# A two-layer transformer kernel: a third tile turned by VectorE, Q projected in halves, the ratio and V's copy on ScalarE, V's bias folded into the output's bias

## What is computed

```python
Q = einsum('bse,hec->bhsc', X, Wq) + bq;  K = ... Wk + bk;  V = ... Wv + bv
Q1, Q2 = Q[..., :d], Q[..., d:];  K1, K2 = K[..., :d], K[..., d:]
A1 = Q1 @ K1.T * s;  A2 = Q2 @ K2.T * s                  # each 1024 x 1024
P = softmax(A1) - lam * softmax(A2)
O = P @ V;  Y = concat(O) @ Wo + bo
return layernorm(Y) * gamma + beta, scaled by 0.2
```

## Time and profile before

| | |
|---|---|
| median of three runs | 1576.91 us (1574.72 to 3416.54) |
| the profiled execution | 1573.77 us, span of its instructions 1572.0 us |
| TensorE clock granted, mean | 0.967 |
| busy PE / DVE / ACT / POOL | 1439.6 / 1376.4 / 1198.3 / 1003.8 us |
| share of the span | 92% / 88% / 76% / 64% |
| DMA | 110.80 MB, mean 70 GB/s |

### The profile page before, as it was taken

How to read it: one execution, slowest core, us unless ns; L and a number is a source line. 1 busy time by engine, 2 the same in 40 slices (tenths; PEclk the granted TensorE clock), 3 DMA queues, 4 the chain that set the end, 5 groups by cost and what they waited for, 6 DMA issues and landing times.

```text
span 1572.0 us, 28031 instructions
## 1 busy us (share of the span) xinstructions
PE 1439.6 (92%) x10243; PEld 588.5 (37%) x10243; DVE 1376.4 (88%) x2107; ACT 1198.3 (76%) x1911; POOL 1003.8 (64%) x727
## 2 busy tenths in 40 slices
PE   5899999999999999999999999986685999999985
PEld 1434443344434443344334433434541222222223
DVE  6798998999899989999999989988687999999947
ACT  4787888888888888888888888874342888888882
POOL 2999998898898988989889889880032011111112
PEclk9999999999999999999999999997696999999997
DMA  4243433343244323433343333420000110000001
GB/s 126 76 105 92 106 86 82 102 112 90 78 103 110 96 77 104 109 92 85 91 107 105 83 91 93 114 68 1 1 22 21 31 35 15 16 16 16 16 16 34
DMA packets 154641, 110.80 MB, mean 70 GB/s; under 512 B 31381, under 2 KB 142906, under 8 KB 154506
## 3 DMA queue, kind: packets, MB, share of 16 engines
q1 hardware_dynamic: 154378, 108.99, 26.5%
q0 software_dynamic: 128, 0.03, 0.0%
HBM read 53.82 MB, written 34.87 MB: 56 GB/s over the span
## 4 chain that ended last, share of the span: by engine, by line
PE 53%; ACT 14%; DVE 13%; issue 11%; POOL 7%; DMA 1%; SPq 0%; POOLq 0%; ACTq 0%; DVEq 0%
PE PS L1573 14%; PE PS L1585 10%; PE PS L1599 9%; ACT ering L847 7%; PE PS L1980 4%; POOL ering L656 3%; DVE nmx L1152 2%; PE PS L1942 2%; DVE region L1172 2%; PE PS L1632 2%; PE PS L1964 2%; ACT region L871 2%; DVE mxp L1479 2%; ACT ering L1059 2%; POOL ering L655 2%
## 5 line engine op out<-in xcount | busy, mean ns | idle before, releaser
L1152 DVE TENSOR_REDUCE nmx<-PS 128x1 f32<-128x1024 f32 x512 | 620.1, 1216 | 54.4 <-PE PS L1574 53.5
L847 ACT ACTIVATE ering<-PS,nmx 128x1024 f32<-128x1024 f32 x512 | 570.6, 1116 | 109.6 <-DVE nmx L1152 109.5
L656 POOL TENSOR_TENSOR ering<-ering 128x1024 f32<-128x1024 f32 x256 | 604.2, 2360 | 21.4
L1573 PE MATMUL PS<-region 64*128 64x512 f16 x1536 | 405.1, 381 | 20.4 <-ACT ering L847 14.5
L1574 PE MATMUL PS<-region 64*128 64x512 f16 x1536 | 405.2, 381 | 0.0
L655 POOL TENSOR_SCALAR ering<-ering,rho 128x1024 f32<-128x1024 f32 x256 | 287.3, 1122 | 95.2 <-DVE rho L1161 94.5
L1479 DVE TENSOR_REDUCE mxp<-PS 128x2 f32<-128x1024 f32 x256 | 304.2, 1222 | 34.3 <-PE PS L1964 29.9
L1059 ACT ACTIVATE ering<-PS 128x1024 f32<-128x1024 f32 x256 | 259.6, 1024 | 70.0 <-PE PS L1942 64.1
L1585 PE MATMUL PS<-ident,ering 128*128 128x128 f32 x1536 | 251.5, 286 | 15.6 <-ACT t L858 8.1
L1585 PEld LDWEIGHTS PS<-ident,ering 128*128 128x128 f32 x1536 | 161.6, 141 | 201.7 <-issue 73.8
L1573 PEld LDWEIGHTS PS<-region 64*128 64x128 f16 x1536 | 112.6, 94 | 261.3 <-ACT ering L847 110.2
(11 more groups left out here) (301 smaller groups left out, 1876.2 us busy)
## 6 DMA issues: line engine op xcount, KB each, us to landing
ptd<-t SPq DMA_DIRECT2D x256, 128.0 KB, 2.4
region<-region SPq DMA_DIRECT2D x64, 256.0 KB, 3.5
t<-ptd SPq DMA_DIRECT2D x44, 256.0 KB, 3.5
region<-ptd SPq DMA_DIRECT2D x44, 256.0 KB, 3.5
va<-ptd SPq DMA_DIRECT2D x20, 256.0 KB, 3.4
acc<-ptd SPq DMA_DIRECT2D x20, 256.0 KB, 3.5
osb<-scr SPq DMA_DIRECT2D x32, 128.0 KB, 3.3
rcp<-scr SPq DMA_DIRECT2D x32, 128.0 KB, 3.3
```

The source lines that it names most:

```text
L656: P.tensor_tensor(e1, e1, e2, ALU.subtract).then_inc(s_sub_ok, 1)
L847: A.activation((E1, E2)[p][s % 4], PS[:, bank:bank + 2, :].rearrange("p a b -> p (a b)"), ACT.Exp, bias=nmx[:, 2 * s + p:2 * s + p + 1], s ...
L1152: V.tensor_reduce(nmx[:, 2 * s + p:2 * s + p + 1], PS[:, bank:bank + 2, :].rearrange("p a b -> p (a b)"), AX.X, ALU.max, negate=True).then ...
L1573: MM(PS[:, bank, :], top[0:64, ql, q], KT[b][0:64, p, kl, :], start=(j == 0), stop=(j == 2))
```

## The change

Its parts, in the order of the code:

- `BY_DVE` becomes (0, 1, 2): DVE turns tile 1 too, in stage 4, and PE's two halves of tile 1 with ACT's two copies are gone. `stage` and `ptd` are used in rotation; SP stores and loads a third tile.
- The ring becomes regular: 17 turns per item, 16 blocks and one for the output product. The Q projection leaves it: `project_q` runs in two halves of 512 columns through `TRB`, in stages 3 and 4 (before: whole, in stage 2). The first half waits until all turned halves of the item before have been copied out, the second until `low_q` of the first has run. `high_q` stands at the end of ACT's stages 3 and 4, `low_q` behind the first maximum of DVE's stages 4 and 5. PE's first turn of an item (now tile 3) waits for `low_q` of both. `swap_q` moves on SP from the item's start to behind the stores of tile 1.
- rho of tiles 2, 3, 4, 6 and 7 is computed by ACT (`ratio`, a 128 x 1 ACTIVATE behind the first exponential of the next stage); lam is then multiplied in by POOL's scaling, which takes two per-partition scalars for these tiles.
- V is copied from PSUM by ACT at the start of stage 0 (before: DVE, with the bias). The biases of all heads go through all of Wo in one chain of eight one-column products in item 0 (`bias_v`), and `bias_out` makes bo + (1 - lam) Wo bv the bias of the output. The loads of Wo whole and of bv as columns take the place of that of `bv_b`.
- `normalise` reads the spread reciprocals without a stride; for that `spread_r` writes single numbers of 4 bytes (before: runs of four).
- POOL splits Wq and Wk with one copy and one subtraction for both (before: two of each).
- `PIECES` becomes {3: (0, 1, 2), 4: (3, 4), 5: (5, 6), 6: (7,)}.

The diff, cut to its core:

```diff
-        BY_DVE = (0, 2)
+        BY_DVE = (0, 1, 2)
+        BY_ACT = (2, 3, 4, 6, 7)
...
-        def ring(v):
-
-
-            at = v + (1 if v >= 1 else 0) + (1 if v >= 5 else 0)
-            return 2 * (at % 3)
-
-        Y_PAIR, Q_PAIR = 2, 0
+        def turn_of(n, v):
+            return 17 * n + v + (1 if v >= 1 else 0)
+        def ring(n, v):
+            return 2 * (turn_of(n, v) % 3)
+        def y_pair(m):
+            return 2 * ((turn_of(m + 2, 1) - 1) % 3) if m + 2 < last0 else 2
+        def q_done(m, i):
+            return 2 * m + i if m else 1
+        def q_place(m, i):
+            if m == 0:
+                return PS[:, 0:2, :].rearrange("p a b -> p (a b)"), slice(0, T)
...
+                             allow_slow_non_contiguous=True).then_inc(s_row_dma, 16)
...
                     store_blocks(n, 1)
+                    if n + 1 < last0:
+                        swap_q(n + 1)
                     load_turned(n, 1)
+                    store_blocks(n, 2)
+                    load_turned(n, 2)
...
-                link(P.tensor_scalar(e2, e2, rho[:, s:s + 1], 1.0, ALU.mult, ALU.mult))
+                link(P.tensor_scalar(e2, e2, rho[:, s:s + 1], cols[:, LAM:LAM + 1] if s in BY_ACT else 1.0, ALU.mult,
+                                     ALU.mult))
...
+            def ratio(n, s):
+                act.wait_ge(s_rr_ok, 8 * n + s + 1)
+                if s > 0 or n > 0:
+                    act.wait_ge(s_rho_ok, 8 * n + s)
+                A.activation(rho[:, s:s + 1], sums[:, s, 0:1], ACT.Identity, scale=rr[:, n % 2, 1, s:s + 1],
+                             bias=0.0).then_inc(s_rho_ok, 1)
...
+            def high_q(m, i):
+                src, at = q_place(m, i)
+                act.wait_ge(s_q_mm, q_done(m, i))
                 at_least(act, s_fill, 16 * (m - 1))
-                A.activation(QT[m % 2][:, 0, :], PS[:, Q_PAIR:Q_PAIR + 2, :].rearrange("p a b -> p (a b)"),
-                             ACT.Identity, bias=bqk[:, m // 2, 0:1]).then_inc(s_qhi_ok, 1)
+                A.activation(QT[m % 2][:, 0, at], src, ACT.Identity, bias=bqk[:, m // 2, 0:1]).then_inc(s_qhi_ok, 1)
...
+            def keep_v(v):
+                p, b, i = v // 4, v // 2 % 2, v % 2
+                act.wait_ge(s_v_mm, v + 1)
+                if v >= 4:
+                    at_least(act, s_pv_mm, v - 2)
+                A.activation(v_slot(p, b, i), MISC.rearrange("p (k d) -> p k d", k=4), ACT.Copy).then_inc(s_v_ev, 1)
...
+                    if (own if s else prv) and (s + 7) % 8 in BY_ACT:
+                        ratio(n if s else n - 1, (s + 7) % 8)
...
+                    if s in (3, 4) and nxt and own:
+                        high_q(n + 1, (3, 4).index(s))
...
+                if s in BY_ACT:
+                    return
...
+                V.tensor_tensor(on[:, :], MISC, RB[n % 2][:, :], ALU.mult).then_inc(s_on_ok, 1)
...
+            def bias_out():
+                dve.wait_ge(s_ld_l0, 32)
+                link(V.tensor_scalar(cols[:, OML:OML + 1], cols[:, LAM:LAM + 1], -1.0, 1.0, ALU.mult, ALU.add))
+                dve.wait_ge(s_bv_mm, 1)
+                V.scalar_tensor_tensor(out=cols[:, BOV:BOV + 1], in0=TRB[:, 0:1], scalar=cols[:, OML:OML + 1],
+                                       in1=cols[:, BO:BO + 1], op0=ALU.mult, op1=ALU.add).then_inc(s_bo_ok, 1)
...
+                    if s in (4, 5) and nxt and own:
+                        low_q(n + 1, (4, 5).index(s))
...
-                elif v == 7 and n + 1 < last0:
-                    pe.wait_ge(s_qlo_ok, n + 2)
-                elif v in (1, 2, 5, 6):
+                elif v in (1, 2):
...
+                if (s, i) == (BY_PE[0], 0) and n + 1 < last0:
+                    pe.wait_ge(s_qlo_ok, 2 * (n + 1) + 1)
...
+                    at_least(pe, s_tr_ev, turned(m - 1, 0))
+                    if i == 1:
+                        pe.wait_ge(s_qlo_ok, q_done(m, 0))
+                for k in range(2) if m == 0 else (i,):
+                    at = slice(m % 2 * T + k * HF, m % 2 * T + k * HF + HF)
...
+            def bias_v():
+                pe.wait_ge(s_ld_bv, 32)
+                pe.wait_ge(s_qlo_ok, q_done(1, 1))
+                for k in range(H0 // 2):
+                    mm = MM(TRB[:, 0:1], wo_all[:, k, :], bv_col[:, k:k + 1], start=(k == 0), stop=(k == H0 // 2 - 1))
+                mm.then_inc(s_bv_mm, 1)
...
-            PIECES = {3: (0, 1, 2), 4: (3,), 5: (4, 5, 6), 6: (7,)}
+            PIECES = {3: (0, 1, 2), 4: (3, 4), 5: (5, 6), 6: (7,)}
...
-                    if s == 2 and nxt and own:
-                        project_q(n + 1)
+                    if s == 3 and nxt and own:
+                        project_q(n + 1, 0)
...
+                    if s == 4 and nxt and own:
+                        project_q(n + 1, 1)
+                    if (n, s) == (0, 5):
+                        bias_v()
```

More of the change, by code:

```diff
@@ L878, in _ @@
                     m = n if s >= 3 else n - 1
+                    if s == 0 and 1 <= n <= last0 - 2:
+                        keep_v(n + 1)
                     if s == 2 and nxt and own:
@@ L1249, in _ @@
                         add_out(n - 2)
[L1250 to L1253 removed]
+                    if own and s - 3 in BY_DVE:
+                        turn_blocks(n, BY_DVE.index(s - 3))
+                    if (n, s) == (0, 5):
+                        bias_out()
                     if (n, s) == (1, 5):
@@ L1593, in values @@
                 if j == 0:
-                    pe.wait_ge(s_ptr_dma[n % 2], 64 * (n // 2 + 1))
+                    c = len(BY_DVE) * n + len(BY_DVE) - 1
+                    for i in range(2):
+                        pe.wait_ge(s_ptr_dma[i], 32 * ((c - i) // 2 + 1))
                 if j % 4 == 0:
@@ L1612, in to_out, with project_q @@
                     r = slice(64 * half, 64 * half + 64)
-                    mm = MM(PS[:, Y_PAIR + half, :], wo_s[r, :], on[r, :], start=True, stop=True)
+                    mm = MM(PS[:, y_pair(n) + half, :], wo_s[r, :], on[r, :], start=True, stop=True)
                 mm.then_inc(s_y_mm, 1)
-            def project_q(m):
+            def project_q(m, i):
                 if m < 2:
```

153 lines of the change are left out of this document (69 added, 84 removed).

## The result

The changed kernel took 1870.62 us (median; 1864.95 to 1871.81) where the kernel before took 1577.36 on the same chip: a ratio of 1.186, 95% interval 1.182 to 1.189. That is 293 us slower, against the 42 us that were forecast, and outside the range of 1566 to 1640. The profiled execution spans 1863.1 us, against 1572.0 for the profiled execution of before.

A forecast was written before the change was run, and what follows sets the result against it. No engine had much to spare, so the order in which the four hand blocks on was taken to decide. Per item 17.2 + 11.9 + 4.1 = 33.2 against 31.76, +42 us on 1573.8: 1616 us, range 1566 to 1640.

The forecast's parts named there:

- the sum: Period per item: 17.2 + 11.9 + 4.1 = 33.2 us against 31.76, so +1.4, 30 times, +42 us.
- rival C: POOL becomes the bound (+82 us, 1656), or 4-byte writes on SP make swap_q late; chance 0.12 for both.
- The three legs: The item's period of 31.76 us, split into stretches led by PE, ACT and PE; forecast 33.2 with DVE leading the first.
- Leg 1: From the first fill of stage 4 (t = 0) to exponential (7,1): 16.2 us before, forecast 17.2, led by DVE.
- Leg 2: From exponential (7,1) to the end of the copy of tile 7's second half, led by ACT: 12.0 us before, forecast 11.9.
- Leg 3: From tile 7's last copy to the next first fill of stage 4, led by PE: 3.5 us before, forecast 4.1.
- the 0.48: ACT's wait for DVE between exponential (7,1) and tile 7's last copy, beside 0.31 for PE; forecast to go in part.
- wait of project_q's second half: In stage 4, PE waits 1.1 us for low_q of the first half, ready at t = 4.4.
- A: ACT takes up its part of the delay, only DVE's floor holds: period 31.5 to 32.3, 1566 to 1590 us; chance 0.27.
- B: PE's loss of 1.2 us per item passes through if DVE keeps up: period 30.6, -35 us, 1539 us; chance 0.13.
- C's half on POOL: A second pointer doubles POOL's scaling of 1.12 us: 34.5 per item, +82 us, 1656 us; within the chance of 0.12.
- C's half on SP: 4-byte writes hold SP ahead of swap_q; over 2.5 us more would delay every item; within the chance of 0.12.

The follow-up runs named there:

- experiment 1: Changed kernel with the reciprocals written in 128 runs of 16 bytes again and normalise strided again: 1636.63 us, ratio 1.040 to the kernel before.
- Experiment 2: Changed kernel with the reciprocals written in 256 runs of 8 bytes and normalise reading by a matching pattern: 1687.26 us, ratio 1.072 to the kernel before.
- Experiment 12: Kernel before with only V's part: V copied by ACT, its bias put into the output's bias by products in item 1: 1582.24 us, ratio 1.0047.
- experiment 8: On top of experiment 1, fill (3,1) put ahead of the Q product and the values in stage 3: 1577.36 us, ratio 1.0019 to the kernel before.
- Experiment 7: On top of experiment 1, the ratios of tiles 2, 3, 4, 6 and 7 taken back to DVE: 1646.36 us, ratio 1.046 to the kernel before.

## Why the prediction was wrong, and where it was right

**The step that failed** is the last one of the change's parts: the spread's 4-byte writes. They had no term in the sum. The prediction saw the place ("its 4-byte writes hold SP", "swap_q, moved behind it and behind six more transfers"), the condition ("over 2.5 us more would delay every item") and the row that bore on it, and then gave it a share of rival C's 0.12, without a price. Three things were wrong in that.

- *The size.* The write goes from 128 pieces to 512. The row of before gave 2.02 for 128. Its bounds were 2.02, if the bytes decide, and four times that, 8.1, if the pieces do. Measured: 7.8. The ratio, at 0.1 to 0.27 us, had a bound on both sides; this cost, whose bounds are 6 apart, had none. With the upper bound the swap starts at t = 10 + 6 = 16, lands at about 20, and the sum has +4 per item, 1736. That, and the range up to it, was in reach from the rows. It would still have been 135 us short, for the two reasons that follow.
- *The margin.* "Over 2.5 us more" came from a swap that starts at 10, lands 3.5 later, and is wanted at 16.1. But the swap is two transfers, and the second starts at t = 11.0, with 1.21 of issue and 4.0 to land (experiment 1): 15 to 16. The margin is under 1 us, and at 16 bytes 10 fills already wait for it, for 9.6 us in all. Experiment 2 shows the rest: 1.7 us more in the write ahead of the swap, 1.7 more per item.
- *What follows the delay.* PE ran at its lower clock after its wait, 1.4 in the item shown. With the delay of fill (0,0), 6.8 (t = 22.82 against 16.04), that is 8.2, which is the difference of the two periods shown, 41.65 - 33.44. The item shown is a little worse than most, since the loads and stores behind its write were slower by 2.0 us together. The mean periods differ by 7.8 (41.39 - 33.63), which gives 233 us over 30 items, and 234 were measured.

The chance was wrong for the same reason: a mechanism with its place, its queue and its condition named doesn't belong into a bag with another that has nothing to do with it.

**The three legs** held, as experiment 1 shows, since it differs from the forecast's case only in the write and in normalise's stride. Leg 1, from the mark to exponential (7,1): 17.4 there (541.07 - 523.70), 16.95 in the changed kernel (638.50 - 621.55), where normalise has no stride; forecast 17.2. Leg 2, 11.8 (507.63 to 519.43 in the item before): forecast 11.9. Leg 3, 4.27 (519.43 to 523.70): forecast 4.1. The period was 33.44 against 33.2, and DVE's work from maximum (3,1) to maximum (7,1) 14.94 in the changed kernel (621.75 to 636.69) against 15.3. What the forecast left out is in two places. The mean period is 33.63 and not 33.44, since some of the fills (0,0) wait for the swap; 1.86 x 30 = 56 of the 62 us over before. Most of the rest is in the first two items: between their exponentials (7,1) lie 37.8 us in experiment 1 (64.38 to 102.21) and 32.6 before (63.21 to 95.76). The prediction had only bias_v there, at under a microsecond. Experiment 12 shows that V's part by itself costs 8.4 in these two items (there with its products in item 1).

The term of leg 2 came out, but not by its working. The text takes off "part of the 0.48", the sum takes off 0.8, which is all of both waits. That V's copy alone cost nothing per item in experiment 12, where 0.2 was expected, also says that ACT had more room there than the legs allow.

**Single prices.** The prices of operations are distances from one start to the next. Two of them came out below the lower bound that the prediction gave them: normalise (0.66) and the reciprocal (0.08).

| | forecast | measured |
|---|---|---|
| maximum (7,1) starts, t | 15.5 | 15.14 |
| fill (0,0) would start, t | 16.1 | 15.96 |
| wait of project_q's second half | 1.1 | 1.17 |
| normalise without stride | 0.66 | 0.59 |
| reciprocal alone | 0.13 | 0.06 |
| ratio on ACT | 0.2 | 0.18 |
| V's copy on ACT | 0.49 | 0.48 |
| POOL's second pointer, per tile | 0 | 0.08 |

The ratio's distance is 637.84 to 638.02 in ACT's timeline of the changed kernel. It agrees with the estimate of 0.19 that the prediction made from the Trainium skill (ScalarE: Activation LUTs, section "What ACT_TABLE_LOAD costs"), for which it had no row.

**The rivals.** A, ACT taking up its part of the delay of leg 1, fell: leg 2 had two waits to give, and V's copy and the ratio used them up (11.8 us, with 0.27 of a wait left, at 515.58 in experiment 1). B, PE's relief passing through, fell as the change stands, and experiment 8 shows what it needs: fill (3,1) ahead of the queries' product. Even then it reached before's time, not 1539. So the advice cited with it, to offload a saturated DVE's work to ScalarE (Trainium skill, Perfetto Trace Analysis, section "Optimizing Scalar/DVE Operations"), brought little in this kernel. Experiment 12 has it alone for V: no change of the regular item, and +7 us in all. Experiment 7 has it for the ratios: -10 us, 0.3 per item, in stages in which DVE leads. C's half on POOL fell: the second pointer adds 79 ns (1193 against 1114), not 1120. C's half on SP is what happened.

## What to carry to other kernels

When a change puts a transfer behind others on a queue, or makes its pieces smaller, write down for each transfer behind it when it starts, lands and is wanted, with the unknown landing at both of its bounds; a margin of 1 us in such a list is worth more attention than all of the engines' prices. A wait of a queue costs nothing by itself: 8 to 9 us cost nothing at the item's start, and 7.8 cost 234 us in all ahead of the swap. And when an engine is relieved without the kernel getting faster, look at what stands at the head of its queue at that moment: moving one fill gave 59 us back here, and the same move cost 70 where that fill had another wait. Where an item repeats some 30 times, read its mean period and the first items apart: a few us more can be a price per item or one paid once, and experiment 12 was the second, where the first had been expected.

## What the runs showed of the hardware

- A transfer of 2 KB from SBUF to DRAM took a time that goes with its pieces: 1.9 us (the kernel before) to 2.6 (experiment 1) for 128 of 16 bytes, 4.0 for 256 of 8, 7.9 for 512 of 4, in medians. Single ones took 1.4 to 4.8, 3.0 to 5.8 and 7.1 to 9.5. Whether the number or the size of the pieces decides is not shown.
- Single issues of SP took far longer than the same issue mostly does: a load of a turned tile 0.62 in the median and 2.4 at the most in the changed kernel, 0.62 and 1.9 in experiment 1. In the item shown two such issues followed the 4-byte write, but they stand in both kernels, so nothing shows that it causes them.
- After a wait of 6.9 us on PE the granted clock was 0.50 (1.2 GHz) in the stretch 644 to 648, in which its work began again, 0.93 in 648 to 652, and 1.00 from there on. In the item shown PE's work from fill (0,0) to fill (0,1) took 4.14 us, and 2.59 in experiment 1, which has no such wait. Over the whole profiled execution the clock was 0.91, against 0.97 there.
- A second per-partition scalar made a TENSOR_SCALAR on POOL over 128 x 1024 slower by 79 ns of 1114.
